# Four record and place buffers instead of two in the edge sort of a graph network kernel

## The chip, the cores and the metric

The kernel runs on one core of one Trainium2 chip. The metric is the device time of one execution in microseconds (us), lower being better. The core has a matrix engine (TensorE, PE in the rows), a vector engine (VectorE, DVE), a scalar engine (ScalarE, ACT), a general engine (GpSimd, POOL) and a sequencer for transfers (SyncE, SP). Each works through its own list of instructions, and they wait for each other on semaphores.

## The reference

Two layers of a graph network over 6,250 nodes with 128 features and 200,000 edges. An edge has a source, a destination and 64 attributes. The first layer is an attention over the edges of each source node; the second passes the features of both ends and the attributes through a small network and sums by source node:

```
h = jnp.maximum(_layernorm(x, axis=-1), 0.0)
x = x + _L0_gnn_ref(h, edge_index, ...)     # softmax over the edges of a row, message to its column
h = jnp.maximum(_layernorm(x, axis=-1), 0.0)
# _L1_gnn_ref:
msg = jnp.concatenate([x[row], x[col], edge_attr], axis=-1)
h = jax.nn.relu(msg @ W1 + b1)
msg_out = h @ W2 + b2
out = jax.ops.segment_sum(msg_out, row, num_segments=x.shape[0])
```

The edges come in sorted by destination. The kernel needs them sorted by source, and so it sorts them itself; the change is in that sort.

## The kernel before

The program is a row of stages, each a block that all engines enter together and leave together. The first prepares features, digits of the indices and prefix counts. The sort is the second large one. Then come the softmax, the aggregation of the first layer, and the gather stage of the second layer, in which GpSimd fetches rows by indirect transfers (`g_q<-q_d,g_rec`) and in which some 40% of the time is spent.

The sort walks NG = 196 groups of GE = 1,024 edges: 8 edges (G) on each of 128 partitions. For each edge it needs a place in the sorted list, and it writes the edge's record of REC = 72 numbers (64 attributes, 4 scores, keys and indices; 288 bytes) to that place in HBM, the tensor `rec_d`. For group g:

- SyncE (`load`) fetches digit rows and prefix counts, two groups deep (`hx_row`, `low_row`, `pre`).
- VectorE (`prepare`) turns them into one-hot rows: one `hx` instruction (L585) and two `low` instructions (L588).
- TensorE matches edges with one another (`rk`, L638 and L642) and looks up the counts and scores (`lk`, L652 to L655), eight slots to a group in four banks. It starts group g+1 only as the readers of `rk` and `lk` free them, one bank after another.
- ScalarE (`group`) first waits until the scatters that last used this record buffer have landed (`s_sc`), starts the load of 64 attributes into the record (L537), and then turns the two halves of `rk` into `equal` (L543).
- VectorE (`finish`) sums `equal` to `rank` (L602), reduces the four banks to `look` (L605, four times, with the next group's `table`, L594, between), then waits for the same `s_sc`, fills the record's other fields (L612, L613, L615) and adds up `place` (L616), which announces the record (`s_rec`). Right behind it comes the `prepare` of a later group.
- GpSimd (`scatter`) waits for `s_rec` and for the attributes (`s_ea`), and issues G = 8 indirect scatters of 128 records each (L561). At the beginning of the stage it has 49 other scatters to issue (`head_d<-head`, L552), and its 1,568 record scatters start behind them.

What matters for the change is the depth of `rec` and `place`: two buffers, one for even and one for odd groups. ScalarE and VectorE can't begin to fill the record of group g before all 8 scatters of group g-2 have landed. The other tiles (`rank`, `look`, `equal`, `hx`, `low`, `tab`) have two buffers as well, and are freed by VectorE and TensorE and not by the scatters. The order of work on each engine is that of the code; there is no scheduler.

Of the kernel before, what the change touches and what calls it, by code (L numbers as in the profile page):

```python
# [59 lines left out]
def pairs(eng, body, n):  # L60

    body(0, 0)
    body(1, 1)
    with eng.Fori(1, n // 2) as i:
        body(i * 2, 0)
        body(i * 2 + 1, 1)
    if n % 2:
        body(n - 1, 0)


def first(k, n=1):

    return isinstance(k, int) and k < n
# [28 lines left out]
def build(nc, x, src, dst, src_t, dst_t, ea, W, att, bias, W1, b1, W2, b2, out):  # L102
    dram = lambda name, shape, dt: nc.dram_tensor(name, shape, dt).ap()
    rec_d = dram("rec_d", (SLOTS, REC), F32)
# [8 lines left out]
    ea_v = ea.rearrange("(g p j) f -> g p j f", p=P, j=G)  # L113

    with ExitStack() as top:
        def sb(name, shape, dt, ctx=top):
            return ctx.enter_context(nc.sbuf_tensor(name, shape, dt))
# [4 lines left out]
        def sem(name):  # L122
            return top.enter_context(nc.semaphore(name))
# [15 lines left out]
        with ExitStack() as edges:  # L139
# [348 lines left out]


            with ExitStack() as ctx:  # L490
                NBANK = G // 2
                hx_row = sb("hx_row", [P, 2, GE], BF16, ctx)
                hx = sb("hx", [P, 2, GE], BF16, ctx)
                low_row = sb("low_row", [P, 2, 2, GE], BF16, ctx)
# [3 lines left out]
                equal = sb("equal", [P, 2, HG, P], BF16, ctx)  # L498
                rank = sb("rank", [P, 2, G], F32, ctx)
                look = sb("look", [P, 2, G, HF], F32, ctx)  # L500
                place = sb("place", [P, 2, G], I32, ctx)
                rec = sb("rec", [P, 2, G, REC], F32, ctx)
                minus_two = sb("minus_two", [P, 1], F32, ctx)
                rk = [pb(f"rk{k}", ctx) for k in range(2)]
                lk = [pb(f"lk{k}", ctx) for k in range(NBANK)]
                s_ld = [sem(f"group_loaded{k}") for k in range(2)]
                s_sc = [sem(f"group_scattered{k}") for k in range(2)]
                s_ea = [sem(f"attributes_loaded{k}") for k in range(2)]
                s_hx, s_low, s_tab = sem("digits_ready"), sem("low_onehot_ready"), sem("table_ready")
                s_rk, s_eq, s_rank = sem("digits_matched"), sem("equal_ready"), sem("rank_ready")  # L510
                s_lk, s_red, s_rec = sem("looked_up"), sem("lookup_reduced"), sem("record_ready")
# [19 lines left out]

                @block.scalar
                def _(act):
                    def group(g, par):
                        if not first(g, 2):
                            act.wait_ge(s_sc[par], (g - par) * (8 * G))
                        act.dma_start(rec[:, par, :, 0:ED], ea_v[bass.ds(g, 1), :, :, :].rearrange("o p j f -> (o p) j f")  # L537
                                      ).then_inc(s_ea[par], 16)
                        for k in range(2):
                            act.wait_ge(s_rk, g * 2 + (k + 1))  # L540
                            if not first(g):
                                act.wait_ge(s_rank, (g - 1) * 2 + (k + 1))
                            act.activation(equal[:, k, :, :].rearrange("p j q -> p (j q)"), rk[k][:, :], ACT.Relu,  # L543
                                           bias=minus_two[:, 0:1]).then_inc(s_eq, 1)

                    act.wait_ge(s_m2, 1)
                    pairs(act, group, NG)

                @block.gpsimd
                def _(pool):  # L550
                    for a in range(NB):
                        pool.indirect_dma_start(head_d, bass.IndirectOffsetOnAxis(ap=head_i[:, a:a + 1], axis=0),  # L552
                                                head[:, a, :], None).then_inc(s_heads, 16)

                    def scatter(g, par):
                        pool.wait_ge(s_rec, g + 1)
                        pool.wait_ge(s_ea[par], (g - par) * 8 + 16)
                        pool.sem_inc(s_go, 1)
                        n = P if not isinstance(g, int) or g < NG - 1 else LAST
                        for j in range(G):  # L560
                            pool.indirect_dma_start(rec_d, bass.IndirectOffsetOnAxis(ap=place[0:n, par, j:j + 1], axis=0),  # L561
                                                    rec[0:n, par, j, :], None).then_inc(s_sc[par], 16)

                    scatter(0, 0)
                    scatter(1, 1)
                    with pool.Fori(1, NG // 2 - 1) as i:
                        scatter(i * 2, 0)
                        scatter(i * 2 + 1, 1)
                    scatter(NG - 2, 0)
                    scatter(NG - 1, 1)  # L570
                    pool.wait_ge(s_heads, 16 * NB)
                    pool.wait_ge(s_sc[0], 8 * G * NG)
                    pool.wait_ge(s_sc[1], 8 * G * NG)

                @block.vector
                def _(v):
                    v.memset(minus_two[:, :], -2.0).then_inc(s_m2, 1)
                    v.tensor_copy(tab[:, 1, G - 1, :], base[:, :]).then_inc(s_m2, 1)
                    v.wait_ge(s_m2, 2)

                    def prepare(g, par):
                        v.wait_ge(s_ld[par], (g - par) * 56 + 112)
                        if not first(g, 2):
                            v.wait_ge(s_lk, (g - 1) * NBANK)
                        v.tensor_scalar(hx[0:R_END, par, :], hx_row[0:R_END, par, :], digit[0:R_END, 0:1], None, ALU.is_equal  # L585
                                        ).then_inc(s_hx, 1)
                        for s in range(2):
                            ins = v.tensor_scalar(low[:, par, s, :], low_row[:, par, s, :], part[:, 0:1], None, ALU.is_equal)  # L588
                        ins.then_inc(s_low, 1)

                    def table(g, par):
                        if not first(g):
                            v.wait_ge(s_tab, g)
                        v.tensor_tensor(tab[:, par, :, :], pre[:, par, :].rearrange("p (j a) -> p j a", j=G),  # L594
                                        row(tab[:, 1 - par, G - 1, :], P, G, NB), ALU.add).then_inc(s_tab, 1)

                    def finish(g, par, last=False):
# [12 lines left out]
                        if not first(g, 2):  # L610
                            v.wait_ge(s_sc[par], (g - par) * (8 * G))
                        v.tensor_copy(rec[:, par, :, F_KEY:F_DST + 1], meta[:, one, :, :].rearrange("p o j f -> p (o j) f"))  # L612
                        v.tensor_copy(rec[:, par, :, F_IDX].bitcast(I32), dst_i[:, one, :].rearrange("p o j -> p (o j)"))  # L613
                        v.wait_ge(s_red, g * NBANK + NBANK)
                        v.tensor_copy(rec[:, par, :, F_SD:F_SD + HEADS], look[:, par, :, 1:HF])  # L615
                        v.tensor_tensor(place[:, par, :], look[:, par, :, 0], rank[:, par, :], ALU.add).then_inc(s_rec, 1)  # L616

                    prepare(0, 0)
                    table(0, 0)
                    prepare(1, 1)  # L620
                    finish(0, 0)
                    prepare(2, 0)
                    finish(1, 1)
                    with v.Fori(1, NG // 2 - 1) as i:
                        prepare(i * 2 + 1, 1)
                        finish(i * 2, 0)
                        prepare(i * 2 + 2, 0)
                        finish(i * 2 + 1, 1)
                    prepare(NG - 1, 1)
                    finish(NG - 2, 0)  # L630
                    finish(NG - 1, 1, last=True)

                @block.tensor
                def _(pe):
# [669 lines left out]
```

## Time and profile before

| | us |
|---|---|
| median of 3 runs (lowest to highest) | 6182.07 (6180.73 to 6191.53) |
| the profiled execution, its own time | 6198.27 |
| span of the profiled execution | 6196.5 |
| scatters of the sort, first start to last start | 475.3 to 2595.4 |
| entry of the sort (first `head_d` scatter) | 411.8 |
| first instruction of the next stage | 2607.3 |

The rows below are from the profile of that one execution. "Busy" is the time an engine spends in instructions, and "idle" is the time ahead of an instruction in which the engine had none, put down to what released it ("issue": nothing that the profile shows). The span of a GpSimd scatter in the rows is the making of its transfer, not the transfer's movement of data.

### The profile page before, as it was taken

How to read it: one execution, taken by the hardware profiler on the slowest of the kernel's cores; microseconds unless marked ns; L12 is line 12 of the kernel's file. 1: busy time of each engine (PE TensorE's matmuls, PEld its weight loads, DVE VectorE, ACT ScalarE, POOL GpSimd, SP SyncE). 2: the span in 40 equal slices, each digit the busy share in tenths (PEclk: the TensorE clock that was granted, in tenths of full speed). 3: DMA queues.
4: the chain of work that ended last, by engine and by line, in shares of the span. 5: the costliest groups of instructions: out<-in, count | busy, mean ns of one | idle time of the engine just before them, and what ended most of it. 6: DMA issues, size and time to landing. Idle time of an engine off the chain costs nothing. (4 is left out here: it accounts for less than half of the span.)

```text
span 6196.5 us, 110907 instructions
## 1 busy us (share of the span) xinstructions
PE 4449.7 (72%) x23829; PEld 3487.0 (56%) x23830; DVE 4123.9 (67%) x7504; ACT 1599.3 (26%) x3277; POOL 3349.7 (54%) x3489
## 2 busy tenths in 40 slices
PE   3656777777777777500299976788888888888886
PEld 3545655666666666400288862566666666666665
DVE  7754555555555555418999976677777777777774
ACT  2421111111111111000166652233333333333332
POOL 1247777777777777500000000677777777777772
PEclk9987888888888888755699988999999999999998
DMA  9834555555555554690000022554555555555556
GB/s 268 307 87 116 131 130 130 135 128 129 135 132 134 131 135 132 89 62 0 0 0 0 0 62 63 151 142 137 140 139 138 139 137 140 137 140 137 140 135 96
DMA packets 1028467, 725.53 MB, mean 117 GB/s; under 512 B 763322, under 2 KB 846068, under 8 KB 1028316
## 3 DMA queue, kind: packets, MB, share of 16 engines
q1 hardware_dynamic: 685932, 391.40, 28.5%
q0 software_dynamic: 131616, 276.04, 15.7%
q10 hardware_dynamic: 210896, 57.82, 3.9%
q8 instruction: 9, 0.15, 0.0%
q14 instruction: 14, 0.11, 0.0%
HBM read 563.05 MB, written 161.88 MB: 117 GB/s over the span
## 5 line engine op out<-in xcount | busy, mean ns | idle before, releaser
L1061 POOL DMA_INDIRECT g_q<-q_d,g_rec x1664 | 1655.6, 995 | 1873.1 <-DMA g_lrow<-low_row_d 1342.4
L561 POOL DMA_INDIRECT rec_d<-rec,place x1568 | 1566.7, 999 | 554.6 <-issue 499.6
L1178 PE MATMUL g_hp<-pw,g_mix 128*128 x3328 | 938.3, 404 | 289.2 <-DVE g_q L1087 247.6
L1098 DVE TENSOR_TENSOR agg<-agg,g_ap 128x256 f32 x1664 | 697.7, 419 | 581.6 <-PE g_ap L1189 444.8
L655 PE MATMUL lk<-tab_sd,low 128*128 128x196 f32 x3136 | 1066.0, 428 | 0.0
L1178 PEld LDWEIGHTS g_hp<-pw,g_mix 128*128 128x128 f32 x3328 | 566.0, 189 | 659.8 <-issue 615.7
L1142 ACT ACTIVATE g_hid<-g_q 128x512 f32<-128x512 f32 x832 | 523.8, 630 | 1517.9 <-DVE g_q L1087 1132.9
L1189 PE MATMUL g_ap<-g_hid,g_oh 128*128 128x256 f32 x3328 | 877.1, 386 | 42.0 <-DVE agg L1098 27.1
L602 DVE TENSOR_REDUCE rank<-equal 128x4 f32<-128x512 bf16 x392 | 253.6, 681 | 919.1 <-ACT equal L543 918.6
L543 ACT ACTIVATE equal<-rk,minus_two 128x512 bf16<-128x512 f32 x392 | 251.4, 684 | 1946.1 <-DMA rec_d<-rec,place 873.3
L1189 PEld LDWEIGHTS g_ap<-g_hid,g_oh 128*128 128x128 f32 x3328 | 599.9, 190 | 190.9 <-issue 119.4
L876 PE MATMUL e_acc<-e_oh_w,e_oh_low 128*128 128x196 f32 x3328 | 595.3, 336 | 118.6 <-DVE e_oh_w L861 118.6
L652 PE MATMUL lk<-mask,hx 122*128 122x245 bf16 x1568 | 489.4, 312 | 263.0 <-DVE tab L594 262.4
L654 PEld LDWEIGHTS lk<-tab,low 128*128 128x128 f32 x3136 | 590.3, 234 | 117.9 <-issue 61.1
L876 PEld LDWEIGHTS e_acc<-e_oh_w,e_oh_low 128*128 128x128 f32 x3328 | 547.1, 190 | 166.6 <-DVE e_oh_w L861 166.6
L654 PE MATMUL lk<-tab,low 128*128 128x49 f32 x3136 | 592.7, 276 | 0.0
L655 PEld LDWEIGHTS lk<-tab_sd,low 128*128 128x128 f32 x3136 | 584.7, 232 | 0.0
L1087 DVE TENSOR_TENSOR g_q<-g_hp,g_q 128x512 f32<-128x512 f32 x832 | 569.3, 684 | 5.6 <-PE g_hp L1178 3.9
L605 DVE TENSOR_REDUCE look<-lk 128x10 f32<-128x490 f32 x784 | 483.5, 658 | 0.0
L638 PE MATMUL rk<-not_below,ident_b 128*128 128x512 bf16 x392 | 170.1, 434 | 326.1 <-ACT equal L543 313.4
L861 DVE TENSOR_TENSOR e_oh_w<-e_oh_high,al 128x1568 f32<-128x1568 f32 x208 | 371.2, 1785 | 0.0
L839 ACT ACTIVATE e_oh_low<-iota,e_minus_low 128x128 f32<-128x128 f32 x832 | 265.8, 390 | 343.7 <-PE e_acc L876 201.6
(222 smaller groups left out, 4499.0 us busy)
## 6 DMA issues: line engine op xcount, KB each, us to landing
low_row<-rows_d SPq DMA_DIRECT2D x392, 256.0 KB
rec_d<-pad SPq DMA_DIRECT2D x64, 936.0 KB, 5.6
g_rec<-rec_d SPq DMA_DIRECT2D x208, 288.0 KB
rec<-in_ea ACTq DMA_DIRECT2D x196, 256.0 KB
hx_row<-rows_d SPq DMA_DIRECT2D x392, 98.0 KB
g_lrow<-low_row_d SPq DMA_DIRECT2D x208, 128.0 KB
g_q<-q_d,g_rec POOLq DMA_INDIRECT x1664
rec_d<-rec,place POOLq DMA_INDIRECT x1568
```

Of the source, the lines that this page charges most:

```text
L561: pool.indirect_dma_start(rec_d, bass.IndirectOffsetOnAxis(ap=place[0:n, par, j:j + 1], axis=0), rec[0:n, par, j, :], None).then_inc(s_sc[ ...
L605: v.tensor_reduce(look[:, par, 2 * b:2 * b + 2, :].rearrange("p j f -> p (j f)"), lk[b][:, 0:2 * LK].rearrange("p (f a) -> p f a", a=NB), ...
L652: pe.matmul(to, hx[0:R_END, par, slots], mask[0:R_END, :], start=True, stop=False, skip_group_check=True)
L654: pe.matmul(to[:, 0:NB], low[:, par, 0, slots], of, start=False, stop=True, skip_group_check=True)
L655: mm = pe.matmul(to[:, NB:LK], low[:, par, 1, slots], tab_sd[:, :, :].rearrange("p h a -> p (h a)"), start=False, stop=True, skip_group_ch ...
L876: mm = pe.matmul(acc[:, 0:HEADS * NB], oh_low[:, par, j, :], oh_w[:, par, j, :, :].rearrange("p h a -> p (h a)"), start=first(g) and j == ...
L1061: pool.indirect_dma_start(qg[:, par, j, :], None, q_d, bass.IndirectOffsetOnAxis(ap=rec[:, par, j, F_IDX:F_IDX + 1].bitcast(I32), axis=0)) ...
L1087: v.tensor_tensor(qg[:, par, 2 * u:2 * u + 2, :], hp[u][:, :].rearrange("p (k f) -> p k f", k=2), qg[:, par, 2 * u:2 * u + 2, :], ALU.add) ...
L1098: v.tensor_tensor(to, to, ap[j // 2 % 2][:, j % 2 * HID:(j % 2 + 1) * HID], ALU.add).then_inc(s_agg, 1)
L1142: act.activation(hid[:, u, :, :], qg[:, par, 2 * u:2 * u + 2, :], ACT.Relu).then_inc(s_hid, 1)
L1178: mm = pe.matmul(hp[u][:, k * HID:(k + 1) * HID], mix[:, par, 2 * u + k, :], pw[:, bass.ds(b[k], 1), :].rearrange("p o f -> p (o f)"), sta ...
L1189: mm = pe.matmul(ap[u % 2][:, k * HID:(k + 1) * HID], oh[:, par, 2 * u + k, :], hid[:, u, k, :], start=True, stop=True)
```

## The change

`rec` and `place` get four buffers, with four semaphores each for "scattered" and "attributes loaded". Group g then reuses the buffers of group g-4. So that each buffer has a fixed number in the code, the loops on ScalarE, GpSimd and VectorE walk four groups per iteration; they walked two. The loops of SyncE and TensorE, and all tiles but these two, stay as they were.

```
+def quads(eng, body, n):
+
+    for k in range(4):
+        body(k, k)
+    with eng.Fori(1, n // 4 - 1) as i:
+        for k in range(4):
+            body(i * 4 + k, k)
+    for k in range(4):
+        body(n - 4 + k, k)
...
-                place = sb("place", [P, 2, G], I32, ctx)
-                rec = sb("rec", [P, 2, G, REC], F32, ctx)
+                place = sb("place", [P, DEEP, G], I32, ctx)
+                rec = sb("rec", [P, DEEP, G, REC], F32, ctx)
...
-                s_sc = [sem(f"group_scattered{k}") for k in range(2)]
-                s_ea = [sem(f"attributes_loaded{k}") for k in range(2)]
+                s_sc = [sem(f"group_scattered{k}") for k in range(DEEP)]
+                s_ea = [sem(f"attributes_loaded{k}") for k in range(DEEP)]
...
-                    def group(g, par):
-                        if not first(g, 2):
-                            act.wait_ge(s_sc[par], (g - par) * (8 * G))
+                    def group(g, at):
+                        if not first(g, DEEP):
+                            act.wait_ge(s_sc[at], (g - at) * (4 * G))
...
-                    pairs(act, group, NG)
+                    quads(act, group, NG)
...
-                        if not first(g, 2):
-                            v.wait_ge(s_sc[par], (g - par) * (8 * G))
+                        if not first(g, DEEP):
+                            v.wait_ge(s_sc[at], (g - at) * (4 * G))
...
-                    with v.Fori(1, NG // 2 - 1) as i:
-                        prepare(i * 2 + 1, 1)
-                        finish(i * 2, 0)
-                        prepare(i * 2 + 2, 0)
-                        finish(i * 2 + 1, 1)
+                    with v.Fori(1, NG // DEEP - 1) as i:
+                        for k in range(DEEP):
+                            prepare(i * DEEP + (k + 1), (k + 1) % 2)
+                            finish(i * DEEP + k, k)
```

On ScalarE, in its loop over the sort's groups, the second group of an iteration and the end of the loop read before (L537 starts the load of attributes, L543 makes `equal`):

```order
L537 ISA [waits group_scattered1]
L537 DMA rec<-in_ea 128x8x64
L540 ISA
L543 ACTIVATE equal<-rk,minus_two 128x512 [waits rank_ready,digits_matched]
L540 REGISTER_ALU
L543 ACTIVATE equal<-rk,minus_two 128x512 [waits rank_ready,digits_matched]
L64 REGISTER_ALU
L64 COMPARE_AND_BRANCH
```

and now its second and third group (L548 is the load, L554 makes `equal`):

```order
L548 ISA [waits group_scattered1]
L548 DMA rec<-in_ea 128x8x64
L551 ISA
L554 ACTIVATE equal<-rk,minus_two 128x512 [waits rank_ready,digits_matched]
L551 REGISTER_ALU
L554 ACTIVATE equal<-rk,minus_two 128x512 [waits rank_ready,digits_matched]
L548 ISA [waits group_scattered2]
L548 DMA rec<-in_ea 128x8x64
L551 ISA
L554 ACTIVATE equal<-rk,minus_two 128x512 [waits rank_ready,digits_matched]
```

The wait for landed scatters still stands ahead of each group's load and `equal`, but it is now for the buffer used four groups earlier.

On GpSimd, the loop that issues the sort's scatters, before:

```order
L566 ISA
L557 ISA [waits record_ready]
L561 DMA rec_d<-rec,place 212992x72 [waits attributes_loaded0]
L561 DMA rec_d<-rec,place 212992x72 x7
L556 REGISTER_ALU
L561 DMA rec_d<-rec,place 212992x72 [waits record_ready,attributes_loaded1]
L561 DMA rec_d<-rec,place 212992x72 x7
L566 REGISTER_ALU
L566 COMPARE_AND_BRANCH
```

and now (its first three groups of four):

```order
L75 ISA
L568 ISA [waits record_ready]
L572 DMA rec_d<-rec,place 212992x72 [waits attributes_loaded0]
L572 DMA rec_d<-rec,place 212992x72 x7
L567 REGISTER_ALU
L572 DMA rec_d<-rec,place 212992x72 [waits record_ready,attributes_loaded1]
L572 DMA rec_d<-rec,place 212992x72 x7
L567 REGISTER_ALU
L572 DMA rec_d<-rec,place 212992x72 [waits record_ready,attributes_loaded2]
L572 DMA rec_d<-rec,place 212992x72 x7
```

GpSimd issues the same scatters with the same two waits at the head of a group; only the number of groups between two branches has doubled.

## Rows read from the trace of the kernel before

**Rows 1.** Window of the sort: PE, PEld, DVE, ACT, POOL busy; PEclk, DMA share, GB/s

```profile
475.00:2597.00 2122.00, 1559.62 (x9650) 1292.90 (x9650) 1200.59 (x2709) 248.66 (x388) 1566.71 (x1569) 0.81 0.51 130
```

**Rows 2.** Groups by line, 475 to 2597: busy, mean ns, idle before, releasers

```profile
L561 POOL DMA_INDIRECT rec_d<-rec,place x1568 | 1566.7, 999 | 554.6 <-issue 499.6 <-DVE place L616 55.1
```

**Rows 3.** Line L561: ns min/median/max, first and last start; idle time until

```profile
L561 POOL DMA_INDIRECT rec_d<-rec,place x1568: 897/958/1471, 475.3 to 2595.4; - x196
...
  DVE place L616: 55.1, 82
```

**Rows 4.** Waits, 475 to 2597: total us, times, longest

```profile
ACT equal L543 <- DMA rec_d<-rec,place: 873.3, 92, 12.4
ACT equal L543 <- PE rk L642: 163.7, 41, 9.1
```

**Rows 5.** Timeline, a head that waits: start, us, engine, [idle before]

```profile
494.47 1.01 POOL L561 DMA_INDIRECT rec_d<-rec,place  x1 [0.30 <-issue]
...
500.57 0.55 ACTq L537 DMA_DIRECT2D rec<-in_ea  x1
501.29 1.26 ACT L543 ACTIVATE equal<-rk,minus_two 128x512 bf16<-128x512 f32 x2 [12.36 <-DMA rec_d<-rec,place]
...
504.62 0.96 POOL L561 DMA_INDIRECT rec_d<-rec,place  x1 [0.31 <-issue]
...
506.23 0.16 DVE L616 TENSOR_TENSOR place<-look,rank 128x8 int32<-128x8 f32 x1
...
507.22 0.96 POOL L561 DMA_INDIRECT rec_d<-rec,place  x1 [1.64 <-DVE place L616]
```

**Rows 6.** Timeline, first and last loads behind the scatters that free them

```profile
484.14 0.96 POOL L561 DMA_INDIRECT rec_d<-rec,place  x1 [0.30 <-issue]
...
486.85 0.60 ACTq L537 DMA_DIRECT2D rec<-in_ea  x1
...
2575.62 0.96 POOL L561 DMA_INDIRECT rec_d<-rec,place  x1 [0.30 <-issue]
...
2577.98 0.55 ACTq L537 DMA_DIRECT2D rec<-in_ea  x1
```

**Rows 7.** GpSimd timeline, 15 scatters without a wait

```profile
1482.56 0.95 POOL L561 DMA_INDIRECT rec_d<-rec,place  x1 [0.30 <-issue]
...
1490.12 1.45 POOL L561 DMA_INDIRECT rec_d<-rec,place  x1 [0.30 <-issue]
1491.88 0.96 POOL L561 DMA_INDIRECT rec_d<-rec,place  x1 [0.30 <-issue]
...
1500.72 0.96 POOL L561 DMA_INDIRECT rec_d<-rec,place  x1 [0.30 <-issue]
```

**Rows 8.** GpSimd timeline, first and last of 13 long stalls

```profile
629.24 0.95 POOL L561 DMA_INDIRECT rec_d<-rec,place  x1 [4.56 <-issue]
...
2453.12 0.96 POOL L561 DMA_INDIRECT rec_d<-rec,place  x1 [3.98 <-issue]
```

**Rows 9.** VectorE and GpSimd timeline, the last prepare and its scatter

```profile
2564.89 1.40 DVE L588 TENSOR_SCALAR low<-low_row,part 128x1024 f32<-128x1024 bf16 x2
2565.05 1.43 POOL L561 DMA_INDIRECT rec_d<-rec,place  x1 [0.30 <-issue]
```

**Rows 10.** VectorE timeline, places of the first two groups, no scatter awaited

```profile
431.85 0.16 DVE L616 TENSOR_TENSOR place<-look,rank 128x8 int32<-128x8 f32 x1
...
438.08 0.16 DVE L616 TENSOR_TENSOR place<-look,rank 128x8 int32<-128x8 f32 x1
```

**Rows 11.** TensorE timeline, two slots at the lower clock

```profile
1501.25 0.99 PE L655 MATMUL lk<-tab_sd,low 128*128 128x196 f32 x2
...
1502.54 0.99 PE L655 MATMUL lk<-tab_sd,low 128*128 128x196 f32 x2
```

**Rows 12.** Page, costliest groups: an add of the gather stage's VectorE loop

```profile
L1087 DVE TENSOR_TENSOR g_q<-g_hp,g_q 128x512 f32<-128x512 f32 x832 | 569.3, 684 | 5.6 <-PE g_hp L1178 3.9
```

More of the change, by code:

```diff
@@ L490, in build @@
             with ExitStack() as ctx:
-                NBANK = G // 2
+                NBANK, DEEP = G // 2, 4
                 hx_row = sb("hx_row", [P, 2, GE], BF16, ctx)
@@ L533, in _ @@
                 def _(act):
-                    def group(g, par):
-                        if not first(g, 2):
-                            act.wait_ge(s_sc[par], (g - par) * (8 * G))
-                        act.dma_start(rec[:, par, :, 0:ED], ea_v[bass.ds(g, 1), :, :, :].rearrange("o p j f -> (o p) j f")
-                                      ).then_inc(s_ea[par], 16)
+                    def group(g, at):
+                        if not first(g, DEEP):
+                            act.wait_ge(s_sc[at], (g - at) * (4 * G))
+                        act.dma_start(rec[:, at, :, 0:ED], ea_v[bass.ds(g, 1), :, :, :].rearrange("o p j f -> (o p) j f")
+                                      ).then_inc(s_ea[at], 16)
                         for k in range(2):
@@ L553, in _, with scatter @@
                                                 head[:, a, :], None).then_inc(s_heads, 16)
-                    def scatter(g, par):
+                    def scatter(g, at):
                         pool.wait_ge(s_rec, g + 1)
-                        pool.wait_ge(s_ea[par], (g - par) * 8 + 16)
+                        pool.wait_ge(s_ea[at], (g - at) * 4 + 16)
                         pool.sem_inc(s_go, 1)
@@ L560, in scatter @@
                         for j in range(G):
[L561 to L570, printed above, removed]
+                            pool.indirect_dma_start(rec_d, bass.IndirectOffsetOnAxis(ap=place[0:n, at, j:j + 1], axis=0),
+                                                    rec[0:n, at, j, :], None).then_inc(s_sc[at], 16)
+                    quads(pool, scatter, NG)
                     pool.wait_ge(s_heads, 16 * NB)
-                    pool.wait_ge(s_sc[0], 8 * G * NG)
-                    pool.wait_ge(s_sc[1], 8 * G * NG)
+                    for at in range(DEEP):
+                        pool.wait_ge(s_sc[at], 4 * G * NG)
                 @block.vector
@@ L595, in table, with finish @@
                                         row(tab[:, 1 - par, G - 1, :], P, G, NB), ALU.add).then_inc(s_tab, 1)
-                    def finish(g, par, last=False):
+                    def finish(g, at, last=False):
+                        par = at % 2
                         for k in range(2):
@@ L609, in finish @@
                         one = bass.ds(g, 1)
-                        if not first(g, 2):
-                            v.wait_ge(s_sc[par], (g - par) * (8 * G))
-                        v.tensor_copy(rec[:, par, :, F_KEY:F_DST + 1], meta[:, one, :, :].rearrange("p o j f -> p (o j) f"))
-                        v.tensor_copy(rec[:, par, :, F_IDX].bitcast(I32), dst_i[:, one, :].rearrange("p o j -> p (o j)"))
+                        if not first(g, DEEP):
+                            v.wait_ge(s_sc[at], (g - at) * (4 * G))
@@ L614, in finish @@
+                        v.tensor_copy(rec[:, at, :, F_KEY:F_DST + 1], meta[:, one, :, :].rearrange("p o j f -> p (o j) f"))
+                        v.tensor_copy(rec[:, at, :, F_IDX].bitcast(I32), dst_i[:, one, :].rearrange("p o j -> p (o j)"))
                         v.wait_ge(s_red, g * NBANK + NBANK)
-                        v.tensor_copy(rec[:, par, :, F_SD:F_SD + HEADS], look[:, par, :, 1:HF])
-                        v.tensor_tensor(place[:, par, :], look[:, par, :, 0], rank[:, par, :], ALU.add).then_inc(s_rec, 1)
+                        v.tensor_copy(rec[:, at, :, F_SD:F_SD + HEADS], look[:, par, :, 1:HF])
@@ L618, in _ @@
+                        v.tensor_tensor(place[:, at, :], look[:, par, :, 0], rank[:, par, :], ALU.add).then_inc(s_rec, 1)
                     prepare(0, 0)
                     table(0, 0)
[L620 to L623, printed above, removed]
-                    with v.Fori(1, NG // 2 - 1) as i:
-                        prepare(i * 2 + 1, 1)
-                        finish(i * 2, 0)
-                        prepare(i * 2 + 2, 0)
-                        finish(i * 2 + 1, 1)
@@ L629, in _ @@
-                    prepare(NG - 1, 1)
-                    finish(NG - 2, 0)
-                    finish(NG - 1, 1, last=True)
+                    for k in range(DEEP):
+                        prepare(k + 1, (k + 1) % 2)
+                        finish(k, k)
+                    with v.Fori(1, NG // DEEP - 1) as i:
+                        for k in range(DEEP):
+                            prepare(i * DEEP + (k + 1), (k + 1) % 2)
+                            finish(i * DEEP + k, k)
+                    for k in range(DEEP):
+                        if k < DEEP - 1:
+                            prepare(NG - DEEP + k + 1, (k + 1) % 2)
+                        finish(NG - DEEP + k, k, last=k == DEEP - 1)
```

## The prediction

> **What bounds the kernel now.** The change lies in the sort, so I read that stage by itself. Over its 2,122 us GpSimd is busy for 1,567 us, TensorE for 1,560 and VectorE for 1,201 [rows 1]. Numbers that near decide nothing; the idle time does. GpSimd shows 1,568 scatters with 554.6 us of idle time ahead of them [rows 2], but most of that is no wait. In a quiet stretch, 14 steps from 1482.56 to 1500.72 with one scatter 0.49 us too long, a scatter starts every 1.26 us: 0.96 busy, 0.30 idle [rows 7]. The gaps read 0.30 or 0.31; at 0.305 each, 1,568 of them are 478 us that belong to the issue itself. With the median scatter of 0.958 [rows 3] the floor of GpSimd is 1,568 x 1.263 = 1,980 us. It took 2,121 (475.3 to the end of the scatter begun at 2595.4). The other 141 us come in three parts.
>
> (a) Longer scatters: 1,566.7 - 1,568 x 0.958 = 65 us [rows 2, 3].
>
> (b) Thirteen long stalls. Each stands between the first and the second scatter of a group, 14 groups (112 scatters) after the one before, with 2.17 to 4.56 us idle [rows 8]. Together they are 43.5 us, 39.5 over the normal gap. The program has no wait there.
>
> (c) The rest: 554.6 - 478 - 39.5 = 37 us, ahead of the first scatter of a group. 69 of the 196 heads have over 0.33 us. As a cross-check, 82 heads are put down to `place`, with 55.1 us [rows 3]: 55.1 - 82 x 0.305 = 30 over normal. The missing 7 are heads with a small delay that is called "issue".
>
> **Why a head waits.** One case can be followed step by step [rows 5]. The last scatter of group 1 ended at 495.48. Its data landed so late that ScalarE's load for group 3 began at 500.57, 5.1 us on. `equal` comes 0.72 us behind the load, and `place` ends at 506.39, 5.8 us behind it. GpSimd had ended its last scatter of group 2 at 505.58 and began group 3 at 507.22: 0.83 us behind `place`, after 1.64 us idle in place of 0.31. In the mean over 194 groups the load follows the end of the freeing scatter by 3.3 us (1.4 to 5.4; the first and the last took 1.75 and 1.40 [rows 6]). So a buffer takes 3.3 + 5.8 + 0.8 = 9.9 us from its last scatter to the next one's start, and GpSimd spends 0.3 + 8 x 1.263 = 10.4 on the group between. That's a race won or lost by a little, which fits 69 small waits. The release by landed scatters is ScalarE's largest named wait, 873 us in 92 waits [rows 4].
>
> **The change part by part.**
>
> *The deeper record.* Group g is now released by group g-4, two groups or 20 us sooner. The spread that has to be covered is 2 us at a head and 4.6 at most [rows 5, 8]. What would be late next is production. Where no scatter held it back, one `place` followed the other by 6.2 us [rows 10]. VectorE works 1,200.6/196 = 6.1 us on a group and TensorE 8.0 [rows 1], both under GpSimd's 10.1. So the producers run ahead until four buffers are full, and part (c) goes: -37 us.
>
> *The stalls (b).* Their spacing goes by the count of scatters, which doesn't change, and they are GpSimd's own, so no buffer ahead of GpSimd covers them: 0. They come in two sizes, near 2.2 and near 4.2 us. All small, 13 x 2.2 = 29 in place of 43.5, is -15; all large, 13 x 4.4 = 57, is +14. Those are the bounds.
>
> *The longer scatters (a).* They lie beside the two `low` instructions of a `prepare`: one of 1.43 us began 0.16 us into them [rows 9]. `prepare` follows `place` at once, and `place` follows a landing, so it drifts along GpSimd's scatters. I paired the 195 prepares of the stretch with the scatters that they overlap (the last pair is [rows 9]). Where a waiting head lies in the overlap, 69 times, the excess over 0.96 is 0.235 us in the mean: part of the collision falls into time in which GpSimd waits anyway. In the other 126 it is 0.302. With no waiting heads all have 0.302: 69 x 0.067 = +5 us. So a little of what is won is given back. The lower bound is the mean of the 127 groups whose head doesn't wait, 0.21 us: 196 x 0.21 = 41 against 65, -24. The upper bound is a rival, below.
>
> *The loops.* Half as many branches on three engines. The gap ahead of a head that doesn't wait is the normal 0.30, at the start of an iteration or within it, so a branch is hidden behind the scatter in front of it: 0. Instructions and transfers stay the same in number.
>
> *The ends.* The first record scatter stands behind GpSimd's 49 others, with records ready long before in either kernel [rows 10]. The drain behind the last one stays. 0.
>
> Sum: -37 + 5 = -32 us. The profiled execution took 6,198.3 us (span 6,196.5, and 1.8 around it), 16 above the median of the runs, 6,182.1, a difference that no row puts in the sort. So I take the 32 us off the median: **6,150 us**.
>
> **A rule that speaks against it.** Scatters reach 1.471 us against 0.958 [rows 3], beside VectorE's `low` [rows 9]. The Trainium skill, page "SBUF — State Buffer", section "SBUF: two separate sides", says that while VectorE runs an instruction that takes both port pairs, GpSimd is locked out and can't write the descriptors of its transfers. By that rule the price hangs on the phase alone, and an engine that no longer waits is always there to be locked out; by the rows the sum loses 5 us through it, by the rule's worst case 119 (the rival of the phases). The trace agrees with its direction, 0.302 us without a wait against 0.235.
>
> **The rivals.**
>
> *Nothing comes of it: 6,182.* `place` would be late for TensorE's sake. ScalarE was released by `rk` 41 times, for 164 us [rows 4]. TensorE's granted clock is 0.81 in the mean [rows 1]; at the lower level, 1.2 GHz, a slot takes 1.29 us [rows 11], the eight of a group 10.3, and with the matching more than GpSimd's 10.1. If groups came in long runs at that level, no buffer would help. Against it: TensorE works 8.0 us on a group and is idle for 2.9, and four buffers need only the average to be under 10.1.
>
> *More comes of it: 6,121.* Part (a) at its lower bound, -24 in place of +5: -37 - 24 = -61. With all stalls small as well it would be 6,106.
>
> *Slower, the phases lock: 6,264.* With no head waiting, each `prepare` might fall so that it lengthens two scatters by 0.47 us each (1.43 against 0.96 [rows 9]). That is 196 x 0.94 = 184 us against 65, +119, less 37: +82. It decides from an excess of 0.33 + 37/196 = 0.52 us per group. For it: the 69 groups with a waiting head hold 0.556 us in the mean. Against it: those hold two collisions, at their head and at their end, and the time to the landing varies by 4 us, three scatter steps, which spreads the phase.
>
> *Slower, the branches: 6,352.* If each of the 47 iterations of the longer loops cost GpSimd a stall like the first of [rows 8], 4.3 us over normal, that would be +202 less 32, +170. Against it: the gather stage's VectorE loop has 117 listed instructions, the sort's new one 98, and its L1087 has 5.6 us idle in 832 [rows 12]. The page "Runtime: NRT & Kernel Launch", section "Instruction fetch mechanics", of the Trainium skill is a reason to list it: a taken branch to a target outside the fetched window stalls the engine. No run here shows it.
>
> **How the numbers follow.** The forecast, with a range of its own of 6,135 to 6,164 (the stalls' -15 and +14): 0.64. More: 0.12. Nothing, or nearly so: 0.16. Phases that lock, wholly or in part: 0.06. Branches: 0.02. The range takes in the forecast, the case of more down to 6,118, and the lower half of the case of nothing, up to 6,176. A measurement of this kernel tells about 0.2%, 12 us, from no change. So faster holds 0.64, 0.12 and 0.03 of the third case, 0.79; same the other 0.13; slower 0.08.
>
> **What the profile after would show.** The idle time of the 1,568 scatters falls from 554.6 to about 518 us, next to none of it put down to `place`. Their busy time rises to about 1,572. The 13 stalls are still 112 scatters apart. ScalarE's wait for landed scatters stays large, since it now waits for a full queue, but `place` ends ten or more us ahead of its scatter. The mechanism is wrong if heads still wait with four buffers. The size is wrong if the mean of a scatter leaves 0.99 to 1.01 us, or if the stalls change in number or size.

## The result and the profile after

The changed kernel took 6,105.4 us (median of 4 executions, 6,084.4 to 6,118.0) where the kernel before, run beside it, took 6,184.5: a ratio of 0.9867 [0.9834, 0.9901]. That is 79 us faster. 32 were predicted, and the time lies below the range. A second comparison (e2 below) gave 0.9853 [0.9839, 0.9867].

The page of the changed kernel's profiled execution (span 6,082.6 us), its first part:

```profile
PE 4398.1 (72%) x23829; PEld 3457.8 (57%) x23830; DVE 4119.8 (68%) x7504; ACT 1603.2 (26%) x3277; POOL 3381.1 (56%) x3489
```

The window of its sort, with the columns of [rows 1], its group of scatters as in [rows 2], and the line by itself as in [rows 3]:

```profile
472.00:2511.00 2039.00, 1500.44 (x9550) 1252.26 (x9550) 1187.11 (x2681) 248.89 (x384) 1560.77 (x1569) 0.82 0.52 134
```

```profile
L572 POOL DMA_INDIRECT rec_d<-rec,place x1568 | 1560.7, 995 | 478.0 <-issue 477.7 <-DMA rec_d<-rec,place 0.3
```

```profile
L572 POOL DMA_INDIRECT rec_d<-rec,place x1568: 897/958/1537, 472.4 to 2509.9; - x196
...
  issue: 477.7, 1567
  DMA rec_d<-rec,place: 0.3, 1
```

The idle time is 478.0 us. That is exactly the 478 that the prediction counted as the issue's own, 1,568 gaps of 0.305. So not only the waits for `place` are gone, 82 with 55.1 us in [rows 3], but also the 13 stalls of [rows 8]. The place where the first one stood, GpSimd's timeline of the changed kernel (start, us, engine, [idle before]); the scatter that begins at 618.69 opens the fifteenth group:

```profile
617.42 0.96 POOL L572 DMA_INDIRECT rec_d<-rec,place  x1 [0.30 <-issue]
618.69 1.01 POOL L572 DMA_INDIRECT rec_d<-rec,place  x1 [0.30 <-issue]
620.00 0.95 POOL L572 DMA_INDIRECT rec_d<-rec,place  x1 [0.30 <-issue]
```

The waits of its sort (total us, times, longest), to be held against [rows 4]:

```profile
ACT equal L554 <- DMA rec_d<-rec,place: 1673.9, 183, 42.0
DVE rank L608 <- ACT equal L554: 825.0, 234, 36.7
...
ACT equal L554 <- PE rk L647: 106.9, 53, 9.1
```

ScalarE waits for landed scatters twice as long as before, and it costs nothing: the producers run into a full queue. Behind the first four groups, `place` ends about 22 us (20.0 to 24.5) ahead of its group's first scatter. The last scatter and the next stage's first transfer, the changed kernel and then the kernel before:

```profile
2509.88 0.91 POOL L572 DMA_INDIRECT rec_d<-rec,place  x1 [0.30 <-issue]
2515.11 0.72 SPq L707 DMA_DIRECT2D fld<-rec_d  x1
```

```profile
2595.45 0.90 POOL L561 DMA_INDIRECT rec_d<-rec,place  x1 [0.30 <-issue]
2607.21 0.72 SPq L702 DMA_DIRECT2D fld<-rec_d  x1
```

The drain between the stages has shrunk from 11.8 us to 5.2. And the gather stage, whose code is the same, differs too. Its group in the page, changed kernel, then before:

```profile
L1066 POOL DMA_INDIRECT g_q<-q_d,g_rec x1664 | 1689.5, 1015 | 1807.3 <-DMA g_lrow<-low_row_d 1308.0
```

```profile
L1061 POOL DMA_INDIRECT g_q<-q_d,g_rec x1664 | 1655.6, 995 | 1873.1 <-DMA g_lrow<-low_row_d 1342.4
```

Its gathers have become 34 us longer in sum and their idle time 66 us shorter. Before, 73 heads of groups of eight gathers had 0.4 to 1.7 us idle there, and six stalls of 1.97 or 1.98 us stood 200 gathers apart or a multiple of that. The changed kernel has one such head and no such stall.

The spans, part by part, for this pair of profiles and for the pair e1, e2 (us):

| | before | after | e1 (before) | e2 (after) |
|---|---|---|---|---|
| start to first record scatter | 475.3 | 472.4 | 475.8 | 475.3 |
| first to last record scatter | 2120.1 | 2037.5 | 2121.4 | 2042.9 |
| drain to the next stage's transfer | 11.8 | 5.2 | 11.8 | 5.2 |
| from there to the first gather | 1283.5 | 1279.4 | 1280.7 | 1277.8 |
| first to last gather | 2233.5 | 2212.1 | 2227.8 | 2217.6 |
| tail | 72.4 | 76.0 | 76.6 | 77.1 |

Inside the sort: waiting heads -36.9 and -29.9, stalls -39.5 and -46.3, the scatters' busy time -6.0 and -2.2.

Some experiments ran on chips on which the kernel before itself takes a fifth longer (7,387 to 7,554 us); they stand in a section of their own, with ratios against the kernel before on the same chip.

### The profile page after: what moved, and what is told of

Its sections match the earlier page's. It is cut to its first block and busy times, and to the rows that moved or that the text cites. A ratio compares the mean times of both kernels' runs of the same rounds, so it can differ in the third digit from the quotient of the medians.

```text
span 6082.6 us, 110351 instructions
## 1 busy us (share of the span) xinstructions
PE 4398.1 (72%) x23829; PEld 3457.8 (57%) x23830; DVE 4119.8 (68%) x7504; ACT 1603.2 (26%) x3277; POOL 3381.1 (56%) x3489
## 5 line engine op out<-in xcount | busy, mean ns | idle before, releaser
L1066 POOL DMA_INDIRECT g_q<-q_d,g_rec x1664 | 1689.5, 1015 | 1807.3 <-DMA g_lrow<-low_row_d 1308.0
L572 POOL DMA_INDIRECT rec_d<-rec,place x1568 | 1560.7, 995 | 478.0 <-issue 477.7
L660 PE MATMUL lk<-tab_sd,low 128*128 128x196 f32 x3136 | 1046.2, 421 | 0.0
L554 ACT ACTIVATE equal<-rk,minus_two 128x512 bf16<-128x512 f32 x392 | 254.4, 685 | 1840.5 <-DMA rec_d<-rec,place 1673.9
L659 PEld LDWEIGHTS lk<-tab,low 128*128 128x128 f32 x3136 | 577.1, 230 | 113.8 <-issue 55.0
L660 PEld LDWEIGHTS lk<-tab_sd,low 128*128 128x128 f32 x3136 | 572.2, 228 | 0.0
```

The source lines that it names most:

```text
L659: pe.matmul(to[:, 0:NB], low[:, par, 0, slots], of, start=False, stop=True, skip_group_check=True)
L660: mm = pe.matmul(to[:, NB:LK], low[:, par, 1, slots], tab_sd[:, :, :].rearrange("p h a -> p (h a)"), start=False, stop=True, skip_group_ch ...
L1066: pool.indirect_dma_start(qg[:, par, j, :], None, q_d, bass.IndirectOffsetOnAxis(ap=rec[:, par, j, F_IDX:F_IDX + 1].bitcast(I32), axis=0)) ...
```

## The experiments

**Both kernels again (e1, e2), and the loops alone (e3).** e3 keeps two buffers and two semaphores and takes only the loops of four, on all three engines:

```
-                    pairs(act, group, NG)
+                    quads(act, lambda g, at: group(g, at % 2), NG)
...
+                    quads(pool, lambda g, at: scatter(g, at % 2), NG)
...
+                    with v.Fori(1, NG // 4 - 1) as i:
+                        for k in range(4):
+                            prepare(i * 4 + (k + 1), (k + 1) % 2)
+                            finish(i * 4 + k, k % 2)
```

> The kernel before, unchanged. Ratio 1.000 within 0.2%. Theory A (the 13 long stalls of GpSimd in the sort, 39.5 us over normal, belong to two buffers and a late release): all 13 are there again, 112 scatters apart, and GpSimd's idle time over 1,568 scatters is again about 555 us. Theory B (the stalls come and go from one execution to another, whatever the kernel): their number or size differs from 13 and 43.5 us in this execution, as they did between the traces of before and after, and the time moves with them.

> The changed kernel once more. Theory A: no stall over 1 us among the 1,568 scatters, idle time again 478 us, time 79 us under the kernel before. Theory B: some executions have stalls again; if this one does, idle time is about 478 + 40 us and the time some 40 us more than the fastest run (6,084), which would also explain why four runs spread from 6,084 to 6,118.

> Two buffers as before, but ScalarE, GpSimd and VectorE walk four groups an iteration. If the loops hold the stalls (a matter of GpSimd's branches: 13 stalls in 96 iterations, at the second scatter of an iteration), they change in number with the iterations, to 6 or 7 or none, and the time falls by 20 to 40 us while the waits at the heads of groups (37 us) stay. Under theory A nothing changes: 0 us. Under theory B the stalls differ by chance.

Measured: e1 1.0003 [0.9992, 1.0015], e2 0.9853 [0.9839, 0.9867], e3 0.9964 [0.9952, 0.9977] (6,174.2 us against 6,199.8). In e3 all 13 stalls stand at the same scatters as before, counted from 0 the 113th, 225th and on by 112, with 51.0 us (50.3 in e1), which includes the normal gaps; 62 heads wait, 27 us over normal; the drain is 11.8. The scatters and the gathers of e3 in its page:

```profile
L572 POOL DMA_INDIRECT rec_d<-rec,place x1568 | 1558.3, 994 | 552.5 <-issue 511.7
...
L1065 POOL DMA_INDIRECT g_q<-q_d,g_rec x1664 | 1689.9, 1016 | 1821.7 <-DMA g_lrow<-low_row_d 1322.3
```

So the loops take away neither waits nor stalls in the sort. But they bring the whole change in the gather stage (1,016 ns, 2,217.3 us from first to last), and the sort's scatters are 10 us shorter in sum than e1's 1,568.3. The stalls of e1 and e3 also take sizes between the two of the prediction, 3.4 us three times in e1.

**Four buffers and semaphores, released as late as before (e4).** Group g waits for group g-2 again, on ScalarE as shown and on VectorE likewise; everything else is the changed kernel:

```
-                        if not first(g, DEEP):
-                            act.wait_ge(s_sc[at], (g - at) * (4 * G))
+                        if not first(g, 2):
+                            act.wait_ge(s_sc[(at + 2) % DEEP], (g - at) * (4 * G) + (at // 2) * (16 * G))
```

> Four buffers and semaphores and the loops of the change, but ScalarE and VectorE still wait for the scatters of two groups ago. The waits at heads should be back as before: 37 us over normal, 65 to 85 heads that wait. Theory A (late release makes heads wait and the stalls too): the time of the kernel before, ratio 1.00. If the stalls hang on the number of buffers, semaphores or loops and not on the release: about 37 us slower than the changed kernel and some 40 us faster than the kernel before.

Measured: 0.9905 [0.989, 0.9919], 6,136.4 us. The heads wait as before, 63 of them with 31.6 us over normal, so the early release is what removes those waits. But the long stalls are gone without it. What is left are shorter pauses, again ahead of the second scatter of a group and now 96 scatters apart or a multiple of that. GpSimd's timeline of e4 shows one behind a head that had waited (first two rows, the head and the scatter behind it), the same place 96 scatters on, where there is none, and one behind a head that had not waited:

```profile
1005.54 1.08 POOL L572 DMA_INDIRECT rec_d<-rec,place  x1 [0.73 <-issue]
1008.37 0.96 POOL L572 DMA_INDIRECT rec_d<-rec,place  x1 [1.75 <-issue]
...
1133.95 0.96 POOL L572 DMA_INDIRECT rec_d<-rec,place  x1 [0.30 <-issue]
1135.21 0.96 POOL L572 DMA_INDIRECT rec_d<-rec,place  x1 [0.30 <-issue]
...
1647.57 1.07 POOL L572 DMA_INDIRECT rec_d<-rec,place  x1 [0.30 <-issue]
1650.39 0.96 POOL L572 DMA_INDIRECT rec_d<-rec,place  x1 [1.75 <-issue]
```

Nine such pauses stand in the sort: 1.71 to 1.81 us behind the five heads that had waited, and 1.59 (three times) and 1.75 us behind four that had not. The drain is 5.2 us. For comparison the first stall of e1, the kernel before once more, with ScalarE's load in between:

```profile
625.12 1.01 POOL L561 DMA_INDIRECT rec_d<-rec,place  x1 [0.30 <-issue]
628.72 0.55 ACTq L537 DMA_DIRECT2D rec<-in_ea  x1
630.36 0.96 POOL L561 DMA_INDIRECT rec_d<-rec,place  x1 [4.23 <-issue]
```

There the head had not waited at all. The load at 628.72 is released by the landing of the group before, and GpSimd goes on 1.64 us behind it. In the kernel before and in e3 the stalls of 2.9 us and more all end 1.63 to 1.65 us behind such a load. That looks like a wait for landed scatters that stands nowhere in the program.

**Four semaphores with two buffers (f1), release by g-3 (f2), double `low` (f3), GpSimd's loop alone (f4).** f1 is e3 (two buffers, loops of four, two semaphores for the attributes) with one difference: its scatters signal four semaphores in turn. f2 is the changed kernel with the release one group later. f3 is the changed kernel with each `low` computed twice, the first time into a spare tile. f4 is the kernel before with the loop of four on GpSimd only:

```
+                s_sc = [sem(f"group_scattered{k}") for k in range(4)]
...
+                            pool.indirect_dma_start(rec_d, ..., rec[0:n, par, j, :], None).then_inc(s_sc[at], 16)
```

```
+                        if not first(g, 3):
+                            act.wait_ge(s_sc[(at + 1) % DEEP], (g - at) * (4 * G) + (at // 3) * (16 * G))
```

```
+                        for to in (spare, low):
+                            for s in range(2):
+                                ins = v.tensor_scalar(to[:, par, s, :], low_row[:, par, s, :], part[:, 0:1], None, ALU.is_equal)
```

```
+                    quads(pool, lambda g, at: scatter(g, at % 2), NG)
```

> Two record and place buffers, loops of four, release by group g-2, four semaphores for the scatters' completion; run again, since on the first chip all kernels took 7,300 to 7,500 us with TensorE slowed down. There its pauses stood 96 scatters apart at 1.82 us at most, and 5.2 us behind the last scatter. Expected on a chip at 6,190: the same, no stall over 1.9 us, head waits of 27 to 37 us, and the time of the run with four buffers and late release, 0.990. If the number of buffers counts after all: 0.996.

> The changed kernel with release by group g-3. No head waits, and so no pause can be seen 96 apart either (in the runs with four semaphores it stood only where the head before it had waited): 478 us idle, 0.985, the time of the changed kernel within 0.2%.

> The changed kernel with each prepare's one-hot instructions done twice. On the slow chip the excess of the 1,568 scatters over 0.958 us was 106 us against 56 to 80 there. Expected: 105 to 130 us against 61 to 67, GpSimd still the bound with no head waits, and 40 to 65 us more than the changed kernel (0.992 to 0.996 of the kernel before). If TensorE or VectorE becomes the bound, heads wait again.

> The kernel before with GpSimd's loop of four groups alone. Sort: 13 stalls 112 apart of 2 to 5 us, waits at heads, 2,110 to 2,121 us. Gather: if GpSimd's place in its program decides, about 2,217 us without head waits and without pauses 200 apart, and 0.997; if VectorE's or ScalarE's does, 2,230 us with them and 1.000.

| | ratio to before (6,189.9) | us | sort's scatters | heads over normal | stalls | drain |
|---|---|---|---|---|---|---|
| f1 | 0.9903 [0.9886, 0.992] | 6130.7 | 2082.4 | 64, 32.6 us | 9 of 1.68 to 1.86 and 3 of 0.5 to 1.2, 96 apart or a multiple | 5.2 |
| f2 | 0.9849 [0.9827, 0.987] | 6098.2 | 2042.6 | none | none | 5.2 |
| f3 | 0.9881 [0.9862, 0.99] | 6119.0 | 2060.1 | none | none | 5.2 |
| f4 | 0.9995 [0.9984, 1.0006] | 6186.5 | 2122.5 | 55, 25.4 us | 13, 112 apart, to 4.97 | 11.8 |

The scatters in the pages of f1, f2, f3 and f4, in this order:

```profile
L574 POOL DMA_INDIRECT rec_d<-rec,place x1568 | 1557.3, 993 | 526.4 <-issue 478.9
```

```profile
L572 POOL DMA_INDIRECT rec_d<-rec,place x1568 | 1565.8, 999 | 478.1 <-issue 455.2
```

```profile
L573 POOL DMA_INDIRECT rec_d<-rec,place x1568 | 1583.4, 1010 | 477.9 <-issue 477.6
```

```profile
L572 POOL DMA_INDIRECT rec_d<-rec,place x1568 | 1574.7, 1004 | 549.0 <-issue 506.5
...
L1066 POOL DMA_INDIRECT g_q<-q_d,g_rec x1664 | 1648.0, 990 | 1886.9 <-DMA g_lrow<-low_row_d 1346.8
```

f1 against e3 changes the scatters' semaphores alone, and the stalls over 1.9 us are gone: that is what removes them. f1 is within 0.0002 of e4: the buffers add nothing to what four semaphores and the loops of four give. f2 is within 0.0004 of e2: one more group of depth does all that two do. f4 leaves everything as it was, the gather stage with 990 ns and its stalls too, so GpSimd's own loop is not the cause there. f3 lengthens the scatters by 17.6 us against f2 (1,583.4 less 1,565.8): their excess over 0.958 goes from 63.7 to 81.3 us, where 105 to 130 had been expected. The instructions beside which they were said to lengthen had been doubled, so `low` is a cause, but far from in proportion.

## On the slowed chips

> Two record and place buffers, loops of four groups, release by group g-2 as before; only the scatters' completion now goes to four semaphores in turn. Theory S (the long stalls and the 11.8 us between the last scatter and the next stage hang on how many semaphores the scatters go round): stalls 96 scatters apart and under 1.9 us, 5.2 us behind the last scatter, and the time of the run with four buffers and late release, 0.990 of the kernel before. Theory M (they hang on the number of buffers in SBUF): 13 stalls of 2 to 5 us, 11.8 us, 0.996 as with the loops alone.

> The changed kernel, but ScalarE and VectorE wait for the scatters of group g-3 in place of g-4. By the reckoning of the prediction one group more than before (10 us) covers the spread of the landings: no head waits, idle time 478 us, and the time of the changed kernel, 0.985, within 0.2%. If the stalls need the full depth to vanish, some of up to 1.8 us come back: up to 10 us slower than the changed kernel.

> The changed kernel with each prepare's two instructions on the one-hot rows done twice (the second pair writes a spare tile that nobody reads): VectorE's work per group rises from 6.1 to 7.6 us, still under GpSimd's 10.1. If longer scatters come from VectorE's instructions beside them, the excess over 0.958 us rises from 61 to 67 us to 105 to 130 us, the mean scatter from 0.997 to about 1.03, and the time by 40 to 65 us (0.993 to 0.996 of the kernel before). If they have another cause: no change of scatter durations and 0.985.

> The kernel before with one edit: GpSimd's loop over the sort walks four groups, while ScalarE and VectorE keep their loops of two. In the run with all three loops changed the sort's stalls and waits stayed and the gather stage was 13 us shorter, without its stalls 200 gathers apart. If that comes from GpSimd's own instructions standing elsewhere in its program: gather 2,217 us and no stalls there, and 0.996 to 0.998. If it comes from VectorE's or ScalarE's program: gather 2,230 us with the stalls, ratio 1.000. The 13 stalls of the sort are expected in either case.

These are the kernels of f1 to f4. Against 7,386.8 us: e5 1.0113 [1.0076, 1.015], e6 0.9997 [0.9971, 1.0023], e7 0.9871 [0.9838, 0.9904], e8 0.9991 [0.9959, 1.0023]. Only e8's ratio came out as expected. The changed kernel itself did not run on such a chip, and of the kernel before there is no trace from one. The window of the sort of e6 (columns as in [rows 1]) and two of its longest waits:

```profile
484.00:3047.00 2563.00, 1726.90 (x9712) 1380.32 (x9711) 1204.95 (x2724) 262.28 (x388) 1568.02 (x1567) 0.72 0.41 108
```

```profile
ACT equal L554 <- PE rk L647: 740.1, 162, 17.6
...
POOL rec_d L572 <- DVE place L622: 529.9, 108, 8.8
```

The clock is 0.72 where it was 0.81 in [rows 1], GpSimd's heads wait for `place` for some 500 us, and ScalarE for TensorE 740, in [rows 4] 164. This looks like the prediction's rival "nothing comes of it" on a chip where its condition holds: TensorE is late, and e6's deeper queue gives nothing. That it can't give anything there is not shown, though: e7, with more work on VectorE and one more group of depth than e6, is 1.3% faster, its heads wait 400 us in place of 497, and I can't say which of its two edits does it. Two head rows with the scatter behind each, GpSimd's timeline of e6 and of g3:

```profile
818.14 1.07 POOL L572 DMA_INDIRECT rec_d<-rec,place  x1 [7.75 <-DVE place L622]
820.97 0.95 POOL L572 DMA_INDIRECT rec_d<-rec,place  x1 [1.75 <-issue]
```

```profile
860.41 1.45 POOL L562 DMA_INDIRECT rec_d<-rec,place  x1 [8.20 <-DVE place L618]
863.42 0.95 POOL L562 DMA_INDIRECT rec_d<-rec,place  x1 [1.56 <-issue]
```

The pause comes back in e6 at 14 of its 16 places 96 apart, 1.75 to 1.87 us, each time behind a head that had waited; at the other two places the head had not. But e4 and f1 have pauses without a waiting head, so that is no rule. Then the parts were taken one by one. g1 is e4 with two scatter semaphores for its four buffers, g3 the kernel before (loops of two) with each group's scatters on two semaphores, four in all, g2 and g4 the loop of four on VectorE alone and on ScalarE alone:

```
+                                                    rec[0:n, at, j, :], None).then_inc(s_sc[at % 2], 16)
```

```
+                s_sc = [[sem(f"group_scattered{k}_{h}") for h in range(2)] for k in range(2)]
...
+                                                    rec[0:n, par, j, :], None).then_inc(s_sc[par][j // HG], 16)
```

> Four record and place buffers and the loops of four, but the scatters' completion on two semaphores and release by group g-2. If only the semaphores hold the stalls: 13 stalls of 2 to 5 us, 112 apart, 11.8 us behind the last scatter, 0.996, like the loops alone. If buffers matter too: stalls under 1.9 us and 0.990.

> The kernel before with VectorE's loop of four groups alone. The sort as before: 13 stalls, 2,110 to 2,121 us. Gather: if VectorE's place in its program decides, 2,213 to 2,218 us without head waits, 0.997; otherwise 2,230 us and 1.000.

> The kernel before with its loops of two, but four semaphores: the first four scatters of a group count on one, the last four on another, so that each is used again two groups later, as before. If the distance in groups to the next use of a semaphore decides: stalls of 2 to 5 us, 112 scatters apart, and 1.000. If the mere number of semaphores does: no stall over 1.9 us, 5.2 us behind the last scatter, and 40 us less, 0.993.

> The kernel before with ScalarE's loop of four groups alone. The sort as before. Gather: 2,213 to 2,218 us and 0.997 if ScalarE's place in its program decides, otherwise 2,230 us and 1.000.

Against 7,554.2 us: g1 0.994 [0.992, 0.9961], g2 0.9946 [0.9926, 0.9967], g3 1.0174 [1.0143, 1.0205], g4 0.9993 [0.9964, 1.0021]. g1, g2 and g4 have 13 stalls, again 112 apart, of 1.7 to 3.9 us; one of g1's, behind a head that had not waited:

```profile
2343.20 0.96 POOL L572 DMA_INDIRECT rec_d<-rec,place  x1 [0.30 <-issue]
2347.30 0.96 POOL L572 DMA_INDIRECT rec_d<-rec,place  x1 [3.14 <-issue]
```

With two semaphores stalls of over 1.9 us are back, with four buffers (g1) or two (g2, g4). g3 has no stall over 1.6 us, only seven pauses of 1.56 us, now 208 scatters apart, and its drain is 11.8. g2 and g3 once more on a chip of this kind, as h2 and h1, gave 0.9947 [0.9926, 0.9969] and 1.0158 [1.013, 1.0187]; h1 shows the same seven pauses and one of 0.75 us, 104 scatters ahead of the first. For h1 0.993 to 0.995 had been expected on a chip like the first, and what g3's semaphores are worth there isn't known.

Why e5 and g3 lose over 1% isn't settled. Most of the loss lies in the sort, where the heads wait longer: 609 us over normal in e5 against 469 in e8, on one chip, and 732 in g3 against 580 in g4, on another. The clock granted in the sort was 0.70 in g3 against 0.71 in g4, but 0.72 in e5 against 0.73 in e8, so it doesn't explain both.

g2 is 22 us faster than g4 in the median (7,509 and 7,531), on the same chip, and that difference lies in the sort too: 2,642.2 us from the first scatter to the last in place of 2,663.8. Their scatters, g2 and then g4, in their pages:

```profile
L561 POOL DMA_INDIRECT rec_d<-rec,place x1568 | 1555.5, 992 | 1096.5 <-DVE place L616 608.0
```

```profile
L572 POOL DMA_INDIRECT rec_d<-rec,place x1568 | 1579.5, 1007 | 1094.4 <-DVE place L627 614.0
```

The idle time is the same within 2 us; the scatters themselves are 24 us shorter. Their gather stages are alike, 3,010.8 and 3,009.3 us (g1 3,009.0, g3 3,005.7), and every run on the slowed chips still has stalls near 1.97 us there, those with all three loops too (e5, e6, e7, g1).

## Why the prediction was wrong, step by step

**The waiting heads, -37: right.** -36.9 in the profile that the number came from, -29.9 in the second pair. None is left, and e4 brings them back by the late release alone. f2 shows that the step bought more depth than was needed.

**The stalls, "their spacing goes by the count of scatters, which doesn't change, and they are GpSimd's own ...: 0": this step failed.** The stalls' 39.5 to 46 us went, more than the forecast's whole gain. The count of scatters doesn't change, but the diff also doubles the semaphores on which the scatters signal, and I read that as bookkeeping. In every run with two such semaphores the 13 stalls are 112 apart (before, e1, e3, f4, e8, g1, g2, h2, g4); in no run with four in turn is there one of over 1.9 us (e4, f1, f2, f3, after, e2, and e5 to e7). Four buffers with two semaphores keep them (g1), loops of four keep them (e3), and e3 with four semaphores loses them (f1). What takes their place are pauses of at most 1.87 us, most of them near 1.75 and behind a waiting head, but not all (e4 has four behind heads that had not waited). In the four traces in which no head waits (after, e2, f2, f3), nothing of them shows. Whether they are then hidden or absent the rows can't say. My bounds, -15 to +14, assumed that all 13 remain; that the stalls change in number stands in the prediction as a sign that its size is wrong.

What GpSimd waits for in a stall is argued, not shown: the end 1.64 us behind the load points to the landing of the group before. Why the period is 112 with two semaphores, 96 with four in turn and 208 or 104 with four split is open.

**The longer scatters, +5: the sign holds for the depth alone.** From e4 to e2 the busy time rises by 11.9 us (1,554.2 to 1,566.1), from f1 to f2 by 8.5. But the loops take 10 off (e3 against e1), so the sum came out at -6.0 and -2.2. Two executions of the changed kernel differ by 5.4 us here, so terms of this size are barely told apart. The mean excess over the prepares of the changed kernel, paired as in the prediction, is 0.24 us (0.28 in e2), not 0.302: that figure of the heads that didn't wait doesn't carry over to a kernel in which none waits. The rival of locked phases, +82, didn't come.

The Trainium skill, page "SBUF — State Buffer", section "SBUF: two separate sides", says of VectorE in a two-port mode and GpSimd that whichever starts first holds the shared port pair for its whole instruction. The trace agrees that a scatter beside `low` is longer (up to 1.537 us against 0.958), but twice the `low` added 28% to the excess (f3) and no more.

**The loops, 0: wrong in the sum, right on GpSimd.** All three together are worth 0.36% (e3), about 22 us; between the profiles of e1 and e3 it is 11.8 in the sort and 10.5 in the gather stage. GpSimd's alone gives nothing (f4), and the gap ahead of its heads that don't wait is 0.30 or 0.31 throughout, so the rival of the branches is out as well. VectorE's loop alone gave 0.9946, on slowed chips, where ScalarE's gave 0.9993; the 22 us between the two lie in the sort, where VectorE's loop comes with shorter scatters (g2 against g4). That goes for every run with the release by group g-2: 1,554 to 1,564 us of scatters with VectorE's loop of four (e3, e4, e5, f1, g1, g2, h2), 1,567 to 1,583 without (before, e1, e8, f4, g3, g4, h1). Why is open. So is the gather stage: GpSimd's loop alone leaves it as it was (f4), on the slowed chips it keeps its stalls whichever loops were changed, and neither VectorE's nor ScalarE's ran alone on a chip like the first.

**The ends, 0: the drain is 6.5 us shorter.** It is 5.2 with four semaphores in turn (e4, f1, f2, after) and 11.8 with two (e3, f4, g1) or with four split (g3). Not explained.

Summed for the pair e1, e2: heads -29.9, stalls -46.3, scatters -2.2, drain -6.5, gather stage -10.2, the rest -3.0, together -98 of a span that fell by 98.2. In time, four semaphores in turn are worth 0.6% (f1 against e3), the earlier release 0.5% (e2 against e4) and the loops 0.4% (e3).

## What to carry to other kernels

A deeper buffer often comes with more semaphores and longer loops, and each of the three can have a price of its own: here the semaphores were worth somewhat more than the depth. A stall that recurs at a fixed count and that no wait in the program explains need not be a constant: look at what it ends behind (here ScalarE's load), and count everything in the diff that touches that event. Once the producers are faster in the mean, one more buffer is enough (f2); where they were late in the mean, the same kernel gained nothing (e6).

## What the runs showed of the hardware

GpSimd's indirect scatters stall at a fixed count that follows the way in which they signal: 2.1 to 5.0 us each 112 with two semaphores (down to 1.7 on the slowed chips), at most 1.87 each 96 or a multiple with four in turn, 1.56 each 208 with four split. In e6 and g3 the smaller pause shows only where GpSimd had waited just before; in e4 and f1 it shows without that too. From the last scatter to the next stage's first transfer it took 11.8 us or 5.2, likewise by the semaphores. And chips differ: the same kernel took 6,190 us on one and 7,387 to 7,554 on others, and the runs traced on those had a granted clock of 0.70 to 0.73 in the sort in place of 0.81.
